# Inverting the attention row sums on VectorE with 32x32 block transposes, in place of logarithm and exponential on ScalarE

## The chip, the cores and the metric

One Trainium2 chip, 8 cores. Each core runs the same program on one element of a batch of 8 (2048 tokens by 1024 features); nothing is passed between cores. The metric is the device time of the slowest core, in microseconds. PE is TensorE, ACT ScalarE, DVE VectorE, POOL GpSimd, SP the engine that issues the DMAs.

## The reference

For each batch element, with E = 1024, 16 heads of 64, T = 2048:

```
xn = layernorm(x)
q, k, v = (xn @ wq.T + bq) / 8, xn @ wk.T + bk, xn @ wv.T + bv
attn = softmax(q @ k.T + causal mask)        # per head, over the keys
s = (attn @ v) @ wo.T + bo
g = silu(xn @ weight.T + pooled(xn) @ disha)
return x + s * g
```

The row sums of the softmax are the denominators that this case is about.

## The kernel before

**Tiling.** Queries are cut into four chunks of 512 (tc 0 to 3), heads into eight pairs (p 0 to 7), keys into blocks of 128. For chunk tc only the first 4 tc + 4 key blocks count. A *unit* is one key block of one pair and chunk: two score matmuls (one per head, 64 rows each) into two PSUM banks of PSS, one exponential on ACT over both into a buffer of PT (six of them), a mask on POOL for blocks on the diagonal, and two value matmuls into the two banks of PSO. Two units are a *batch*. There are 32 pair-and-chunk combinations; k = 8 tc + p counts them.

**Row sums.** The stationary operand of a value matmul is 64 columns of values and 64 columns of ones. So PSO[0:64, 0] holds the unnormalised output of the first head (features by queries), and PSO[64:128, 0] its row sums, the same numbers on all 64 partitions. In bank 1 it is the other way about. Step LNK (L734 to L744) takes the logarithm of both groups of sums on ACT, into the partitions of the outputs they belong to, and one exponential with scale -1 turns them into inverses, in one of two buffers Rb. Step NRM (L691 to L697) multiplies on DVE, once per head (L695, L696), into QA, the input of the output projection. PSO has only one set of banks, so the first value matmul of the next pair waits for both products (L581).

**Fillers.** All other matmuls are *tiles* of 8 matmuls of 512 columns: K, Q, V projections, gate tiles G, output projection O; T is a tile of transposes of the normalised input. They share the two banks of PSF by turns: tile n needs the eviction of tile n - 2 (`bank_free`, L510 to L514 in the tensor program). DVE evicts K (L649), Q (L655), V (L638), O (L669, with two further steps OM at L686 and L690) and most T tiles; ACT evicts G tiles.

**Order.** `schedule()` writes one list of steps, and every engine walks through that list and executes its own steps in that order; there is no other order. Time in it is a count of PE's work (`advance`). `values()` emits PV (the value matmuls of a batch, two batches behind the scores) and, at a pair's end, LNK at once and NRM with a due time 2.3 us later. `evict(n)` puts an eviction into the list right behind its tile's last matmul. Layer norm steps (LNS, LNR, LNA), the sums for the gate weights (WEFF), OM and stores have due times as well; while an NRM is due, most of them are held. Fillers are spread over a pair's batches by ACT's time, save for a block that is put behind the second batch, where the value matmuls of the pair before have just ended: `min(BOUNDARY, 0.45 * quota)` matmuls on top of the share, or 8 where gate tiles stand there. QUOTA is 23, 25, 29 and mostly 37 matmuls a pair for tc 0 to 3. At five places (GATES) ACT changes its table to Silu and back for a burst of G tiles.

Of the kernel before, what the change touches and what calls it, by code (L numbers as in the profile page):

```python
# [6 lines left out]
F32 = mybir.dt.float32  # L7
# [57 lines left out]

GATES = {(1, 5): (0, 1, 2), (1, 7): (3, 4, 5), (2, 2): (6, 7, 8), (2, 7): (9, 10, 11), (3, 1): (12, 13, 14, 15)}

BOUNDARY = 12

WEIGHT = {"T": 2, "LN": 0, "WEFF": 0}  # L70

# [5 lines left out]
def schedule():  # L77

    order, due, tiles = [], [], []
    now = [0.0]  # L80
    burst = [False]
    bs = batches()

    def later(us, *token):
# [2 lines left out]
    def advance(us):  # L87
        now[0] += us
        for d in sorted(x for x in due if x[0] <= now[0]):

            if burst[0] and d[2][0] in ("LNR", "LNA", "XL"):
                continue

            if d[2][0] in ("LNS", "LNA", "WEFF", "WL", "XL") and any(x[2][0] == "NRM" for x in due):
                continue
            due.remove(d)
            order.append(d[2])
# [6 lines left out]
    def evict(n):  # L104
        kind = tiles[n][0]
        order.append(("EV", n) + tiles[n])
        if kind == "Q" and tiles[n][1] * 8 + tiles[n][2] + 3 < 32:
            order.append(("WQK", tiles[n][1] * 8 + tiles[n][2] + 3))
        if tiles[n] == ("Q", 3, 7):
            order.append(("XF",))  # L110
        if kind == "V" and tiles[n][1:] == (NTT - 1, 1):
            order.append(("BO",))
        if kind == "O":
            tt, h = tiles[n][1:]

            wait = max([0.0] + [x[0] - now[0] for x in due if x[2][0] == "NRM"])
            later(wait, "OM", n, tt, h)
            later(wait + 2.2, "ST", tt, h)
            if h == 1 and tt + 2 < 12:
                later(wait + 2.2, "XR", tt + 2)  # L120

    def whole(kind, *which):
        n = tile(kind, *which)
# [6 lines left out]
        evict(n)  # L130

    def ln(tt):
        wait = max([0.0] + [x[0] - now[0] for x in due if x[2][0] == "NRM"])
        later(wait, "LNS", tt)
        later(wait + 2.5, "LNR", tt)
        later(wait + 4.0, "LNA", tt)
        if tt + 2 < NTT:
            later(wait + 5.5, "XL", tt + 2)


    order += [("LNS", 0), ("LNR", 0), ("LNA", 0), ("LNS", 1), ("LNR", 1), ("LNS", 2), ("LNR", 2)]
# [76 lines left out]
    def values(b):  # L218

        tc, p, units = bs[b]  # L220
        order.append(("PV", b))
        advance(sum(2 * (512 - off) for _, _, off in units) / 2400)
        if units[1][1] == 4 * tc + 3:
            k = tc * 8 + p
            order.append(("LNK", k))
            if k < 31:
                later(2.3, "NRM", k)
            return tc, p
        return None

# [2 lines left out]
    for tc in range(NTC):  # L233
        if tc == 3:
            order += [("XR", 0), ("XR", 1)]
        q += fillers(tc)
        for p in range(NPAIR):
            mine = [b for b, x in enumerate(bs) if x[:2] == (tc, p)]
            over += needed(q, [("K", tc, p), ("Q", tc, p)])
            quota = QUOTA[tc][p] - over  # L240

            act = [sum(0.22 + 2 * (512 - off) * 0.83e-3 for _, _, off in bs[b][2]) for b in mine]
            before = (tc, p - 1) if p else (tc - 1, 7)
            extra = 0 if before[0] < 0 else ECH if before in GATES else min(BOUNDARY, 0.45 * max(quota, 0))
            share = [max(quota - extra, 0) * a / sum(act) for a in act]
            due_by, emitted = 0.0, 0
            for i, b in enumerate(mine):
                units = bs[b][2]
                order.extend([("S", b), ("E", b, 0)])
                advance(sum(512 - off for _, _, off in units) / 2400 + 0.2)  # L250
                lag.append(b)
                end = None
                if len(lag) > 2:
                    c, r, old = bs[lag[0]]

                    for u, sc, _ in old:
                        emitted += needed(q, [("V", sc, r // 4)])
                    end = values(lag.pop(0))
                order.append(("E", b, 1))
                if tc == 3 and (p, i) in ((3, 3), (4, 0), (4, 5), (5, 2), (5, 6), (6, 3), (6, 6), (7, 3)):  # L260
                    order.append(("XB",) + xb.pop(0))
                if end in GATES:

                    emitted += needed(q, [("V", 14, 1)]) if tc == 3 and p == 2 else fill(q, ECH)
                    emitted += gate(GATES[end])

                    emitted += fill(q, 5 if tc < 3 else 2)
                due_by += share[i] + (extra if i == 1 else 0)
# [27 lines left out]
def build_program():  # L296
# [46 lines left out]
    o_PT = used  # L343
    PT = [at(f"PT{i}", [NP, 2, 512], F16) for i in range(6)]

    Rb = [at(f"Rb{i}", [NP, 512], F32) for i in range(2)]
    xin = [at(f"xin{i}", [NP, E], F16) for i in range(2)]
    xn = at("xn", [NP, E], F16)
    tri = at("tri_sb", [NP, NP], F16)
# [45 lines left out]
    with ExitStack() as ctx:  # L395
# [16 lines left out]
        s_tile = sem("s_tile")  # L412
        s_ev = {k: sem(f"s_ev{k}") for k in "TVKQGO"}
        s_s, s_exp, s_mask, s_pv = sem("s_s"), sem("s_exp"), sem("s_mask"), sem("s_pv")
        s_lnl, s_rb, s_nrm = sem("s_lnl"), sem("s_rb"), sem("s_nrm")
# [8 lines left out]

        psT = [PSF.ap().bitcast(F16)[:, i, :] for i in range(2)]
        tri2 = bass.AP(tri.ap().tensor, tri.ap().offset, [list(tri.ap().ap[0]), [0, 2], [1, NP]])
        def out_buffer(m):
            return esb[m % 4] if m < 24 else elast[m - 24]

# [77 lines left out]
        def tensor_program(pe):  # L507
# [8 lines left out]
            for t in ORDER:  # L516
# [7 lines left out]
                elif t[0] == "MM":  # L524
                    _, n, a, b = t
                    kind, i, j = TILES[n]
                    if a == 0:
                        bank_free(n)
                        if kind == "V":
                            pe.wait_ge(s_ev["T"], i + 1)  # L530
                            pe.wait_ge(s_wv[j], 16)
                        elif kind in "KQ":
                            pe.wait_ge(s_ev["T"], 4 * i + 4)
                            pe.wait_ge(s_wqk[(8 * i + j) % 3], 16 * ((8 * i + j) // 3 + 1))
                        elif kind == "G":
                            pe.wait_ge(s_weff, 2 * ECH)
                        else:

                            pe.wait_ge(s_nrm, 8 * (i // 4) + 8 - (b < ECH))
                            pe.wait_ge(s_wo, 16)  # L540
                            if bank_of(n) >= 2:
                                pe.wait_ge(s_exp, len(UNITS))
                    elif kind == "O" and i >= 12:
                        pe.wait_ge(s_nrm, 32)
# [27 lines left out]
                elif t[0] == "PV":  # L572
                    tc, p, units = BS[t[1]]
                    for u, sc, off in units:
                        if sc >= 4 * tc:
                            pe.wait_ge(s_mask, int(masks[u]))
                        else:
                            pe.wait_ge(s_exp, u + 1)
                        if sc == 0 and u > 0:

                            pe.wait_ge(s_nrm, 8 * tc + p)  # L581
                        pe.wait_ge(s_ev["V"], nth[tile_no["V", sc, p // 4]] + 1)
                        if u == 0:
                            pe.wait_ge(s_ones, 1)
                        first, last = sc == 0, sc == 4 * tc + 3
                        pe.matmul(PSO[:, 0, off:512], Vp[:, sc, p, 0:128], PT[u % 6][:, 0, off:512],  # L586
                                  start=first, stop=last)
                        pe.matmul(PSO[:, 1, off:512], Vp[:, sc, p, 64:192], PT[u % 6][:, 1, off:512],  # L588
                                  start=first, stop=last).then_inc(s_pv, 1)

        @block.vector
        def vector_program(dve):

            for t in ORDER:
# [96 lines left out]
                elif t[0] == "NRM":  # L691
                    k = t[1]
                    tc, p = k // 8, k % 8
                    dve.wait_ge(s_rb, k + 1)
                    dve.tensor_tensor(QA[tc][0:64, p, :], PSO[0:64, 0, :], Rb[k % 2][0:64, :], ALU.mult)  # L695
                    dve.tensor_tensor(QA[tc][64:128, p, :], PSO[64:128, 1, :], Rb[k % 2][64:128, :],  # L696
                                      ALU.mult).then_inc(s_nrm, 1)  # L697

        @block.scalar
        def scalar_program(act):  # L700
            act.preload_act_table_set(EXP_SET)
            act.wait_ge(s_cst0, 1)
            for t in ORDER:
# [22 lines left out]
                elif t[0] == "E":  # L726
# [3 lines left out]
                    if u >= 6:  # L730
                        act.wait_ge(s_pv, u - 5)
                    act.activation(PT[u % 6][:, :, off:512], PSS[:, 2 * t[2]:2 * t[2] + 2, off:512],  # L732
                                   AF.Exp, bias=neg2[:], scale=0.125).then_inc(s_exp, 1)
                elif t[0] == "LNK":  # L734
                    k = t[1]
                    tc, p = k // 8, k % 8
                    act.wait_ge(s_pv, sum(8 * (4 * c + 4) for c in range(tc)) + (p + 1) * (4 * tc + 4))
                    if k >= 2:
                        act.wait_ge(s_nrm, k - 1)
                    R = Rb[k % 2]  # L740
                    act.activation(R[0:64, :], PSO[64:128, 0, :], AF.Ln)  # L741
                    act.activation(R[64:128, :], PSO[0:64, 1, :], AF.Ln).then_inc(s_lnl, 1)  # L742
                    act.wait_ge(s_lnl, k + 1)
                    act.activation(R[:], R[:], AF.Exp, scale=-1.0).then_inc(s_rb, 1)  # L744

        @block.gpsimd
        def gpsimd_program(pool):
# [82 lines left out]
```

## Time and profile before

| | us |
|---|---|
| median of 3 runs | 613.11 |
| lowest, highest | 582.15, 620.99 |
| profiled execution | 583.26 |
| its span, slowest core | 581.7 |
| spans of the 8 cores | 575.6 to 581.7 |

| engine | busy us | share of the span |
|---|---|---|
| PE | 519.4 | 89% |
| ACT | 398.0 | 68% |
| DVE | 222.9 | 38% |
| POOL | 122.1 | 21% |

The mean granted TensorE clock of the slowest core is 0.991. A matmul's record is longer than the time it holds the engine, since matmuls are pipelined: 512 columns are recorded with 0.38 us, and the next one starts 0.2155 us after it. So the busy share says little on how far PE is from its limit; gaps between starts and the waits say more.

### The profile page before, as it was taken

To read this page: it belongs to the slowest core of one execution; us is meant where nothing else is said; L and a number is where in the kernel's file an instruction comes from. 1 tells how busy PE (TensorE), PEld (TensorE's weight loads), DVE (VectorE), ACT (ScalarE), POOL (GpSimd) and SP (SyncE) were. 2 spreads that over 40 slices of the span, in tenths; PEclk is the share of its full clock that TensorE was granted. 3 is DMA by queue.
4 is the path that set the end of the run, shared out by engine and by line. 5 is a ranking of instruction groups with operands and counts; after the bars stand their busy time and mean duration, and the time that the engine had idled before them with its cause. 6 is when DMAs were issued, how large, how long until landed. Compare 5 with 4: busy or idle time off the path is not lost.

```text
span 581.7 us, 9555 instructions; the slowest of 8 cores (575.6 to 581.7 us)
## 1 busy us (share of the span) xinstructions
PE 519.4 (89%) x2688; PEld 207.9 (36%) x2688; DVE 222.9 (38%) x335; ACT 398.0 (68%) x495; POOL 122.1 (21%) x157
## 2 busy tenths in 40 slices
PE   2889989889979898899999999999998998999896
PEld 1334433333324343333333333433342333333242
DVE  4447566455311230452022212113110635545625
ACT  2256667767655876787688887677748887888650
POOL 0433332221110211011011111010100332252215
PEclk9989999999989999999999999999999999999899
DMA  7933244043111110111010103110205222223113
GB/s 167 282 105 103 91 145 146 19 154 119 37 37 36 38 55 0 55 38 36 1 38 1 42 32 107 39 37 37 74 0 163 72 91 75 91 73 109 61 50 146
DMA packets 17488, 43.68 MB, mean 75 GB/s; under 512 B 2336, under 2 KB 2336, under 8 KB 17056
## 3 DMA queue, kind: packets, MB, share of 16 engines
q1 hardware_dynamic: 17440, 43.07, 23.7%
q8 instruction: 27, 0.44, 0.3%
q14 instruction: 21, 0.17, 0.1%
HBM read 34.67 MB, written 8.39 MB: 74 GB/s over the span
## 4 chain that ended last, share of the span: by engine, by line
PE 62%; ACT 14%; issue 11%; DVE 8%; DMA 3%; POOL 1%; ACTq 0%; SPq 0%; DVEq 0%; POOLq 0%
PE PSF L556 34%; PE PSS L568 10%; PE PSO L586 10%; ACT PT L732 9%; PE PSO L588 7%; DVE QA L696 2%; DVE QA L695 2%; DMA xfirst<-x 2%; DMA wo_sb<-wo 1%; ACT Rb L742 1%; ACT Rb L741 1%; ACT Rb L744 1%; DVE Vp L638 1%; DVE QA L655 1%; PE PSS L556 1%
## 5 line engine op out<-in xcount | busy, mean ns | idle before, releaser
L732 ACT ACTIVATE PT<-PSS,neg 128x1024 f16<-128x1024 f32 (+1 forms) x320 | 299.3, 982 | 110.0 <-PE PSS L568 106.7
L761 POOL TENSOR_TENSOR PT<-PT,tri_sb 128x256 f16<-128x256 f16 x128 | 88.2, 699 | 424.8 <-ACT PT L732 421.0
L556 PE MATMUL PSF<-XG,wqk 128*128 128x512 f16 x512 | 126.2, 383 | 3.9 <-DVE Vp L638 2.2
L586 PE MATMUL PSO<-PT,Vp 128*128 128x512 f16 (+1 forms) x320 | 111.5, 353 | 11.2 <-DVE QA L696 8.9
L568 PE MATMUL PSS<-QA,KT 64*128 64x512 f16 (+3 forms) x640 | 99.4, 353 | 24.4 <-ACT PT L732 17.7
L588 PE MATMUL PSO<-PT,Vp 128*128 128x512 f16 (+1 forms) x320 | 108.9, 350 | 0.0
L556 PEld LDWEIGHTS PSF<-XG,wqk 128*128 128x128 f16 x512 | 49.0, 98 | 58.6 <-issue 7.0
L638 DVE TENSOR_TENSOR Vp<-PSF,bvb 128x512 f16<-128x512 f32 x32 | 22.1, 691 | 117.7 <-PE PSF L556 117.6
L556 PE MATMUL PSF<-wv_sb,XG 128*128 128x512 f16 x256 | 65.9, 384 | 1.1 <-DVE Vp L638 0.7
L568 PEld LDWEIGHTS PSS<-QA,KT 64*128 64x128 f16 x640 | 27.3, 93 | 109.2 <-issue 107.9
L649 DVE TENSOR_SCALAR KT<-PSF,bqk 128x512 f16<-128x512 f32 x32 | 24.0, 750 | 92.4 <-PE PSF L556 92.1
L556 PE MATMUL PSF<-Weff,XG 128*128 128x512 f16 x256 | 56.9, 379 | 2.0 <-DVE Vp L638 1.0
L556 PE MATMUL PSF<-wo_sb,QA 128*128 128x512 f16 x224 | 56.7, 382 | 2.0 <-DMA wo_sb<-wo 1.3
L586 PEld LDWEIGHTS PSO<-PT,Vp 128*128 128x128 f16 x320 | 31.0, 97 | 74.4 <-issue 56.7
L655 DVE TENSOR_SCALAR QA<-PSF,bqk 128x512 f16<-128x512 f32 x32 | 24.0, 750 | 50.5 <-PE PSF L556 50.3
L720 ACT ACTIVATE XG<-PSF 128x512 f16<-128x512 f32 x32 | 19.0, 597 | 30.2 <-PE PSF L556 30.2
L669 DVE TENSOR_TENSOR esb<-PSF,bob 128x512 f32<-128x512 f32 x24 | 16.6, 690 | 55.0 <-PE PSF L556 54.8
L588 PEld LDWEIGHTS PSO<-PT,Vp 128*128 128x128 f16 x320 | 31.4, 98 | 16.0 <-issue 0.7
L556 PEld LDWEIGHTS PSF<-Weff,XG 128*128 128x128 f16 x256 | 24.7, 98 | 33.4 <-issue 4.3
L556 PEld LDWEIGHTS PSF<-wv_sb,XG 128*128 128x128 f16 x256 | 24.7, 99 | 29.6 <-issue 3.8
L556 PEld LDWEIGHTS PSF<-wo_sb,QA 128*128 128x128 f16 x224 | 21.8, 98 | 27.7 <-issue 3.7
L695 DVE TENSOR_TENSOR QA<-PSO,Rb 64x512 f16<-64x512 f32 x32 | 21.7, 679 | 12.6 <-ACT Rb L744 12.5
(39 smaller groups left out, 268.4 us busy)
## 6 DMA issues: line engine op xcount, KB each, us to landing
wqk<-wqk SPq DMA_DIRECT2D x32, 512.0 KB, 3.4
xin<-x SPq DMA_DIRECT2D x24, 256.0 KB, 3.2
out<-esb SPq DMA_DIRECT2D x24, 256.0 KB, 2.0
wbuf<-wT SPq DMA_DIRECT2D x16, 256.0 KB, 3.3
wv_sb<-wv SPq DMA_DIRECT2D x2, 1024.0 KB, 12.3
wo_sb<-wo SPq DMA_DIRECT2D x1, 2048.0 KB, 8.7
out<-elast SPq DMA_DIRECT2D x8, 256.0 KB, 2.4
xfirst<-x SPq DMA_DIRECT2D x4, 256.0 KB, 4.8
```

The source lines that it names most:

```text
L556: ins = pe.matmul(ps(n), l, r, start=ec == 0, stop=ec == ECH - 1)
L568: ins = pe.matmul(PSS[:, 2 * i + h, off:512], KT[64 * h:64 * h + 64, p, sc * NP:(sc + 1) * NP], QA[tc][64 * h:64 * h + 64, p, off:512], st ...
L586: pe.matmul(PSO[:, 0, off:512], Vp[:, sc, p, 0:128], PT[u % 6][:, 0, off:512], start=first, stop=last)
L588: pe.matmul(PSO[:, 1, off:512], Vp[:, sc, p, 64:192], PT[u % 6][:, 1, off:512], start=first, stop=last).then_inc(s_pv, 1)
L638: dve.tensor_tensor(v, ps(n).rearrange("p (a b c) -> p a b c", a=4, b=2), bvb[:, h * 512:(h + 1) * 512].rearrange("p (a b c) -> p a b c", ...
L649: dve.tensor_scalar(KT[:, p, tc * 512:(tc + 1) * 512], ps(n), bqk[:, p:p + 1], None, ALU.add).then_inc(s_ev["K"], 1)
L655: dve.tensor_scalar(QA[tc][:, p, :], ps(n), bqk[:, 8 + p:9 + p], None, ALU.add).then_inc(s_ev["Q"], 1)
L669: dve.tensor_tensor(esb[m % 4][:], ps(n), bob[:, c], ALU.add).then_inc(s_ev["O"], 1)
L695: dve.tensor_tensor(QA[tc][0:64, p, :], PSO[0:64, 0, :], Rb[k % 2][0:64, :], ALU.mult)
L720: act.activation(g, ps(n), AF.Silu).then_inc(s_ev["G"], 1)
L732: act.activation(PT[u % 6][:, :, off:512], PSS[:, 2 * t[2]:2 * t[2] + 2, off:512], AF.Exp, bias=neg2[:], scale=0.125).then_inc(s_exp, 1)
L761: pool.tensor_tensor(a, a, tri2, ALU.mult).then_inc(s_mask, 1)
```

## The change

ACT loses LNK. NRM on DVE becomes seven steps of which six are instructions with work: two block transposes turn the sums over (out of each 32x32 block the first column then holds 32 different sums), a reciprocal works on those 16 columns, and a third transpose, reading each of them 32 times, lays the inverses out over partitions again. Then come the two products. They signal one by one, and the value matmuls of the next pair wait for them one by one. In `schedule()`, NRM stands right behind PV; a flag `soon` holds the steps with due times while the last value matmuls of a pair are near; BOUNDARY is 14; before four of the five gates the block of up to 8 fillers goes.

```diff
-BOUNDARY = 12
+BOUNDARY = 14
@@ advance
-            if d[2][0] in ("LNS", "LNA", "WEFF", "WL", "XL") and any(x[2][0] == "NRM" for x in due):
+            if soon[0] and d[2][0] in ("LNS", "LNR", "LNA", "WEFF", "WL", "XL", "OM", "ST", "XR"):
                 continue
@@ evict (and the same for the steps of ln)
-            wait = max([0.0] + [x[0] - now[0] for x in due if x[2][0] == "NRM"])
-            later(wait, "OM", n, tt, h)
-            later(wait + 2.2, "ST", tt, h)
+            later(0.0, "OM", n, tt, h)
+            later(2.2, "ST", tt, h)
@@ values
-            order.append(("LNK", k))
             if k < 31:
-                later(2.3, "NRM", k)
+                order.append(("NRM", k))
+                soon[0] = False
@@ the loop over batches
+                lag.append(b)
+                soon[0] = len(lag) > 2 and bs[lag[0]][2][1][1] == 4 * bs[lag[0]][0] + 3
                 order.extend([("S", b), ("E", b, 0)])
                 advance(sum(512 - off for _, _, off in units) / 2400 + 0.2)
-                lag.append(b)
@@
                 if end in GATES:
-                    emitted += needed(q, [("V", 14, 1)]) if tc == 3 and p == 2 else fill(q, ECH)
+                    if end == (3, 1):
+                        emitted += needed(q, [("V", 14, 1)])
                     emitted += gate(GATES[end])
@@ buffers
-    Rb = [at(f"Rb{i}", [NP, 512], F32) for i in range(2)]
+    tS = at("tS", [NP, 512], F32)
+    rS = at("rS", [NP, 16], F32)
+    Rb = at("Rb", [NP, 512], F32)
+        spread = bass.AP(rS.ap().tensor, rS.ap().offset, [list(rS.ap().ap[0]), [1, 16], [0, 32]])
@@ tensor program, PV
-                        if sc == 0 and u > 0:
-                            pe.wait_ge(s_nrm, 8 * tc + p)
...
+                        if sc == 0 and u > 0:
+                            pe.wait_ge(s_nrm, 2 * (8 * tc + p) - 1)
                         pe.matmul(PSO[:, 0, off:512], Vp[:, sc, p, 0:128], PT[u % 6][:, 0, off:512],
                                   start=first, stop=last)
+                        if sc == 0 and u > 0:
+                            pe.wait_ge(s_nrm, 2 * (8 * tc + p))
                         pe.matmul(PSO[:, 1, off:512], Vp[:, sc, p, 64:192], PT[u % 6][:, 1, off:512],
@@ vector program, NRM
+                    dve.wait_ge(s_pv, sum(8 * (4 * c + 4) for c in range(tc)) + (p + 1) * (4 * tc + 4))
+                    dve.transpose(tS[0:64, :], PSO[64:128, 0, :])
+                    dve.transpose(tS[64:128, :], PSO[0:64, 1, :]).then_inc(s_turn, 1)
+                    dve.wait_ge(s_turn, k + 1)
+                    dve.reciprocal(rS[:], tS[:].rearrange("p (a b) -> p a b", b=32)[:, :, 0]).then_inc(s_inv, 1)
+                    dve.wait_ge(s_inv, k + 1)
+                    dve.transpose(Rb[:], spread).then_inc(s_rb, 1)
                     dve.wait_ge(s_rb, k + 1)
-                    dve.tensor_tensor(QA[tc][0:64, p, :], PSO[0:64, 0, :], Rb[k % 2][0:64, :], ALU.mult)
+                    dve.tensor_tensor(QA[tc][0:64, p, :], PSO[0:64, 0, :], Rb[0:64, :],
+                                      ALU.mult).then_inc(s_nrm, 1)
@@ scalar program
-                elif t[0] == "LNK":
-                    k = t[1]
-                    tc, p = k // 8, k % 8
-                    act.wait_ge(s_pv, sum(8 * (4 * c + 4) for c in range(tc)) + (p + 1) * (4 * tc + 4))
-                    if k >= 2:
-                        act.wait_ge(s_nrm, k - 1)
-                    R = Rb[k % 2]
-                    act.activation(R[0:64, :], PSO[64:128, 0, :], AF.Ln)
-                    act.activation(R[64:128, :], PSO[0:64, 1, :], AF.Ln).then_inc(s_lnl, 1)
-                    act.wait_ge(s_lnl, k + 1)
-                    act.activation(R[:], R[:], AF.Exp, scale=-1.0).then_inc(s_rb, 1)
```

## Rows read from the trace of the kernel before

**Rows 1.** The page: busy time of PE and ACT, and the chain that ended last.
```profile
PE 519.4 (89%) x2688; PEld 207.9 (36%) x2688; DVE 222.9 (38%) x335; ACT 398.0 (68%) x495; POOL 122.1 (21%) x157
PE 62%; ACT 14%; issue 11%; DVE 8%; DMA 3%; POOL 1%; ACTq 0%; SPq 0%; DVEq 0%; POOLq 0%
```

**Rows 2.** Waits (engine, tile, line <- releaser: us in total, times, longest).
```profile
PE PSS L568 <- ACT PT L732: 17.7, 45, 1.4
...
PE PSO L586 <- DVE QA L696: 8.9, 14, 2.4
...
PE PSS L568 <- DVE QA L655: 5.3, 4, 1.6
...
PE PSF L556 <- DVE Vp L638: 3.9, 6, 0.8
```

**Rows 3.** Groups by form: count | busy us, mean ns | idle us before.
```profile
L655 DVE TENSOR_SCALAR QA<-PSF,bqk 128x512 f16<-128x512 f32 x32 | 24.0, 750 | 50.5 <-PE PSF L556 50.3
L696 DVE TENSOR_TENSOR QA<-PSO,Rb 64x512 f16<-64x512 f32 x32 | 22.2, 694 | 0.4
...
L695 DVE TENSOR_TENSOR QA<-PSO,Rb 64x512 f16<-64x512 f32 x32 | 21.7, 679 | 12.6 <-ACT Rb L744 12.5
L744 ACT ACTIVATE Rb<-Rb 128x512 f32<-128x512 f32 x32 | 20.2, 630 | 3.2 <-ACT Rb L742 0.4
...
L741 ACT ACTIVATE Rb<-PSO 64x512 f32<-64x512 f32 x32 | 19.0, 593 | 10.3 <-PE PSO L588 9.1
L742 ACT ACTIVATE Rb<-PSO 64x512 f32<-64x512 f32 x32 | 18.8, 588 | 0.4
L690 DVE TENSOR_TENSOR esb<-esb,xin 128x512 f32<-128x512 f32 x24 | 18.3, 762 | 4.1 <-DVE esb L686 4.1
...
L618 DVE TENSOR_SCALAR xn<-xin,mv,rstd 128x1024 f16<-128x1024 f16 x12 | 7.4, 614 | 2.0 <-ACT rstd L711 2.0
...
L610 DVE BATCH_NORM_AGGREGATE mv<-st 128x2 f32<-128x12 f32 x16 | 3.3, 209 | 2.6 <-DVE st L606 2.4
```

**Rows 4.** Order of time, 313.7 to 318 us: start, us, engine, line, operands.
```profile
313.75 0.22 PE L588 MATMUL PSO<-PT,Vp 128*128 128x128 f16 x1
...
314.12 0.59 ACT L741 ACTIVATE Rb<-PSO 64x512 f32<-64x512 f32 x1
...
314.94 0.69 DVE L638 TENSOR_TENSOR Vp<-PSF,bvb 128x512 f16<-128x512 f32 x1 [3.96 <-PE PSF L556]
...
316.14 0.68 DVE L695 TENSOR_TENSOR QA<-PSO,Rb 64x512 f16<-64x512 f32 x1 [0.51 <-ACT Rb L744]
316.84 0.69 DVE L696 TENSOR_TENSOR QA<-PSO,Rb 64x512 f16<-64x512 f32 x1
...
317.14 0.61 PE L568 MATMUL PSS<-QA,KT 64*128 64x512 f16 x4
...
317.69 1.11 ACT L732 ACTIVATE PT<-PSS,neg 128x1024 f16<-128x1024 f32 x1 [0.65 <-PE PSS L568]
...
317.78 0.38 PE L586 MATMUL PSO<-PT,Vp 128*128 128x512 f16 x1
```

**Rows 5.** Order of time, 72.6 to 78.3 us.
```profile
72.77 3.40 PE L556 MATMUL PSF<-XG,wqk 128*128 128x512 f16 x15
...
76.75 0.75 DVE L655 TENSOR_SCALAR QA<-PSF,bqk 128x512 f16<-128x512 f32 x1
...
77.75 0.56 PE L568 MATMUL PSS<-QA,KT 64*128 64x512 f16 x4 [1.58 <-DVE QA L655]
```

**Rows 6.** Order of time, 540 to 547.6 us.
```profile
540.09 1.49 DVE L686 TENSOR_TENSOR esb<-esb,XG 128x512 f32<-128x512 f32 x1
541.75 1.39 DVE L690 TENSOR_TENSOR esb<-esb,xin 128x512 f32<-128x512 f32 x1 [0.17 <-DVE esb L686]
...
546.96 0.38 PE L586 MATMUL PSO<-PT,Vp 128*128 128x512 f16 x1 [2.44 <-DVE QA L696]
```

**Rows 7.** Order of time, 565 to 570 us, the kernel's end.
```profile
569.19 0.59 PE L556 MATMUL PSF<-wo_sb,QA 128*128 128x512 f16 x2 [0.69 <-DVE QA L696]
```

More of the change, by code:

```diff
@@ L81, in schedule @@
     burst = [False]
+    soon = [False]
     bs = batches()
@@ L114, in evict @@
             tt, h = tiles[n][1:]
-            wait = max([0.0] + [x[0] - now[0] for x in due if x[2][0] == "NRM"])
-            later(wait, "OM", n, tt, h)
-            later(wait + 2.2, "ST", tt, h)
+            later(0.0, "OM", n, tt, h)
+            later(2.2, "ST", tt, h)
             if h == 1 and tt + 2 < 12:
-                later(wait + 2.2, "XR", tt + 2)
+                later(2.2, "XR", tt + 2)
     def whole(kind, *which):
@@ L132, in ln @@
     def ln(tt):
[L133 to L136, printed above, removed]
+        later(0.0, "LNS", tt)
+        later(2.5, "LNR", tt)
+        later(4.0, "LNA", tt)
         if tt + 2 < NTT:
-            later(wait + 5.5, "XL", tt + 2)
+            later(5.5, "XL", tt + 2)
     order += [("LNS", 0), ("LNR", 0), ("LNA", 0), ("LNS", 1), ("LNR", 1), ("LNS", 2), ("LNR", 2)]
@@ L414, in build_program @@
         s_s, s_exp, s_mask, s_pv = sem("s_s"), sem("s_exp"), sem("s_mask"), sem("s_pv")
-        s_lnl, s_rb, s_nrm = sem("s_lnl"), sem("s_rb"), sem("s_nrm")
+        s_turn, s_inv, s_rb, s_nrm = (sem(n) for n in ("s_turn", "s_inv", "s_rb", "s_nrm"))
         s_mul, s_add, s_addp, s_bog, s_xb = (sem(n) for n in ("s_mul", "s_add", "s_addp", "s_bog", "s_xb"))
@@ L537, in tensor_program @@
                         else:
-                            pe.wait_ge(s_nrm, 8 * (i // 4) + 8 - (b < ECH))
+                            pe.wait_ge(s_nrm, 2 * (8 * (i // 4) + 8 - (b < ECH)))
                             pe.wait_ge(s_wo, 16)
@@ L543, in tensor_program @@
                     elif kind == "O" and i >= 12:
-                        pe.wait_ge(s_nrm, 32)
+                        pe.wait_ge(s_nrm, 64)
                     for ec in range(a, b):
@@ L693, in vector_program @@
                     tc, p = k // 8, k % 8
+                    dve.wait_ge(s_pv, sum(8 * (4 * c + 4) for c in range(tc)) + (p + 1) * (4 * tc + 4))
[5 more added lines that the diff above has]
+                    dve.transpose(Rb[:], spread).then_inc(s_rb, 1)
                     dve.wait_ge(s_rb, k + 1)
-                    dve.tensor_tensor(QA[tc][0:64, p, :], PSO[0:64, 0, :], Rb[k % 2][0:64, :], ALU.mult)
-                    dve.tensor_tensor(QA[tc][64:128, p, :], PSO[64:128, 1, :], Rb[k % 2][64:128, :],
+                    dve.tensor_tensor(QA[tc][0:64, p, :], PSO[0:64, 0, :], Rb[0:64, :],
+                                      ALU.mult).then_inc(s_nrm, 1)
+                    dve.tensor_tensor(QA[tc][64:128, p, :], PSO[64:128, 1, :], Rb[64:128, :],
                                       ALU.mult).then_inc(s_nrm, 1)
```

## The prediction

> **What bounds the kernel now.** I read the page's busy shares and its chain first, then the list of waits, then the groups by form, and then the order of time around one hand-over from a head pair to the next. The page gives TensorE (PE) 89% of the span and ScalarE (ACT) 68%; the chain runs 62% through PE, 14% through ACT, 8% through VectorE (DVE) [rows 1]. So what matters is what makes PE wait. The waits say: 17.7 us for exponentials at the score matmuls (L568), 8.9 us at the value matmuls for the second normalising product (L696), 5.3 us at the score matmuls for an eviction of a Q tile (L655) [rows 2]. DVE itself waits 12.5 us for the inverted sums (L744) [rows 3].
>
> The hand-over at 314 us shows the clean case [rows 4]. The last value matmul of the pair ends at 313.75 + 0.22 = 313.97; call that zero. ACT starts its first logarithm at +0.15. PE meanwhile runs 15 filler matmuls into the two PSF banks, whose tiles have 8 matmuls each, so a tile ends somewhere in them (here after the fourth) and DVE evicts it at 314.94, before the products. The products start at +2.17 and end at +3.56, the next pair's value matmuls start at +3.81: 0.25 after the release. The score matmuls in between started at +3.17 and waited for nothing. ACT, done with its three instructions, runs one exponential and then stands idle 0.65 us. PE loses only some 0.1 us here: the 15 fillers were there to cover the latency, and do.
>
> **What goes from ACT.** 32 times L741, L742, L744 at 0.593 + 0.588 + 0.630 = 1.81 us, 58.0 us in all [rows 3]; ACT falls from 398.0 to 340 us. On PE's path I cost this at nothing: ACT already has idle time behind the three instructions, before the next scores come [rows 4], and in the rest of a pair it works exactly as before. The cover is PE's filler block; if ACT were in fact late there, at most the 17.7 us of waits for exponentials would come back.
>
> **What DVE gets.** Per pair two 64x512 block transposes out of PSUM, a reciprocal on 128x16, one 128x512 transpose, and the same two products. No row shows a DVE transpose. Nearest is L695, 64 partitions by 512 f32 columns out of PSUM, 0.68 us [rows 3]; I take 0.68 for all three. Lower bound: the fastest streaming row, L618, 1024 columns in 0.61, so 0.31 for 512. Upper bound: the slowest 512-column f32 row, 1.39 us [rows 6]. The reciprocal I take at 0.21, like the small aggregate L610 [rows 3]; it cannot be nothing, and a full row would be 0.68. Each step that waits for the one in front costs another 0.17: L690 behind L686 idles 4.1 us in 24 times [rows 3]. So from zero: 0.15, T 0.68 to 0.83, T to 1.53 (0.02 between unlinked ones, as L695 to L696), +0.17+0.21 to 1.91, +0.17+0.68 to 2.76, +0.17+0.68 to 3.61, +0.02+0.69 to **4.32**. DVE busy goes up by 32 x (3 x 0.68 + 0.21) = 72 us to about 295; that is no bound in itself.
>
> The Trainium skill, "VectorE: DVE Perf Modes", section "The three transpose paths", gives 311 ns for a 128x128 bf16 block transpose, and its errata section a fixed part of 151 cycles at 0.96 GHz for one-per-cycle operations. An estimate from these is 311 + 384/0.96 = 711 ns for 512 columns, and 2.5 us more over the kernel than by the row. The same page's "Rules for kernel authors" call the block transpose the fastest within a bank but say to keep the number of chained DVE operations down; here two become six. No row of before can show either.
>
> **The latency alone.** The wait is now split: the first half may start at 3.61 + 0.25 = 3.86, much like 3.81, the second at 4.32 + 0.25 = 4.57. So by latency a pair costs PE about 0.75 us, less where PE's extra fillers (15 become 16 in tc 2 and 17 in tc 3, by min(BOUNDARY, 0.45 quota) and the even share) cover it.
>
> **What is queued behind it.** This is the term that decides. The NRM step used to enter the common order 2.3 us after the values, so that an eviction of a tile ending sooner stood ahead of it on DVE. Now it stands right behind PV in the order, so DVE waits for the last value matmul and then holds everything until 4.32. All evictions of K, Q, V and O tiles of the filler block come behind it. PE has two PSF banks, and `bank_free` makes tile C wait for the eviction of tile A. With r matmuls left in A at zero (1 to 8 alike), B is through at (r + 8) x 0.2155 (15 fillers in a row take 3.40 us with 0.38 for the last [rows 5], so 3.02/14); A's bank is free at 4.32 + 0.02 + 0.75 (L655 [rows 3]) and PE restarts 0.25 later: at **5.34**. PE's order is fixed, so scores and values behind C wait with it. That PE does stand for such an eviction is seen at 76.75: the Q tile's eviction waits behind L696, ends at 77.50, and the score matmuls start at 77.75 after 1.58 us idle [rows 5].
>
> The stall is 5.34 - (r + 8) x 0.2155 where C begins inside the block, else about 0.5 for the split wait:
> - tc 0 and 1, 14 hand-overs without a gate, 15 fillers: C begins for r up to 6 (mean 3.5), stall 2.86; 14 x (0.75 x 2.86 + 0.25 x 0.5) = 31.8.
> - tc 2, 6 of them, 16 fillers: r up to 7 (mean 4), stall 2.75; 6 x (7/8 x 2.75 + 0.06) = 14.8.
> - tc 3, 6 of them, 17 fillers: always, mean r 4.5, stall 2.65; 15.9.
> - 5 gates: the second G tile needs A's bank as well, though ACT evicts the G tiles; 5 x 2.65 = 13.3.
>
> That is 75.8 us, at about 27 places. Off goes what is in the span of before and is now inside or replaced: 8.9 for L696 and 5.3 for L655 [rows 2]. At the end of the kernel the last four O tiles wait for NRM 31; PE idles 0.69 there for L696 already [rows 7], so all of 4.32 in place of 3.56 shows: +0.8. Holding OM, LNS and the like while a hand-over is near (`soon`) spares cases as at 541, where two O steps of 1.49 and 1.39 us stood in front of the products and PE waited 2.44 us [rows 6]; that wait is part of the 8.9. Sum: 75.8 - 8.9 - 5.3 + 0.8 = **+62 us**. The profiled execution took 583.3 us (span 581.7), so 583.3 + 62 = **645 us**. The median of the runs shown is 613.1 (582.2 to 621.0); the profiled one is at their low end, and a median of after may stand above its best in the same way, which the range leaves room for.
>
> The dropped filler block ahead of four gates moves 8 matmuls behind the gate and costs nothing: PE runs G tiles in their place. The two semaphores more, and buffers tS, rS with one Rb in place of two, cost nothing either: the DVE order alone keeps Rb safe. No DMA is moved past another queue's work but the ST and XR issues of O tiles, which no longer wait for NRM.
>
> **Rivals.**
> - *Latency alone.* A's eviction delays nothing, since tiles end late or the banks are ahead. For it: 12 of the 15 fillers can run on two banks. Against: [rows 5]. Price 26 x 0.75 = 19.5, less 8.9: 594 us, within 2%. Chance 0.07.
> - *ACT was the limit (faster).* The mechanism: free of 1.81 us per pair, ACT never makes PE wait and the products come early. It would give back 17.7 + 8.9 = 26.6 us: 557 us. It decides only if the stalls stay under 26.6/27 = 1.0 us, that is if the DVE chain ends by 2.7 us in place of 4.32, for which even transposes of 0.31 (chain end 3.2) are too slow. For it: the chain's 14% through ACT [rows 1]. Chance 0.06.
> - *Quick blocks, or stalls partly absorbed.* Transposes at 0.31 take 3 x 0.37 = 1.1 us off each of 27 stalls: 645 - 30 = 615. Or PE's pause lets ACT get ahead and the 17.7 us go: 627. Chance 0.15.
> - *Slow blocks.* Transposes at 1.39: 3 x 0.71 = 2.1 us more at 27 places, 58 us: 703. Chance 0.06.
> - *The bank wait as summed*, 645 us, between about 630 and 675. Chance 0.66.
>
> The range 612 to 690 takes in the quick and the absorbed case and half the way to the slow one, and leaves out the two others and the far end of the slow one. A measurement tells this kernel from no change at about 2%. Faster 0.06, within 2% 0.06, slower 0.88: the rest and the near-2% edge of the latency case go to slower.
>
> **What would show it.** In the profile of after: three DVE transposes of 0.6 to 0.75 us a pair and the second product ending 4.2 to 4.5 us past the last value matmul; ACT near 340 us busy; PE's waits at the filler matmuls for DVE evictions, now 3.9 us for V tiles [rows 2], at 50 to 80 us in 20 to 27 pieces of 2 to 4 us, with ACT idle longer for scores by as much; waits of score matmuls for exponentials about the same, 15 to 18 us. I am wrong if a transpose is far from 0.68 us, if the PSF waits stay under 20 us, or if the waits for exponentials fall by as much as the PSF waits rise.

## The result and the profile after

The changed kernel takes 691.15 us (median of 4 runs, 686.69 to 696.37), the kernel before 598.0 us (median of 4, 582.15 to 620.99). As a ratio that is **1.187**, 95% interval 1.172 to 1.201; here and below it leaves out executions in which the cores of a die stood at a lower granted clock than the others (here 613 and 621 us of the kernel before, further on 643 and 621 of e8_split and 752 of e11_long_warm), and the kernel before then takes 583 us. The profiled executions are 686.69 and 583.26 us: 103 us more, where the prediction summed 62. The direction and the wait for a bank came out as forecast, the size did not: 691 lies just past the top of the range (690), and a part of it has a cause that the prediction does not name.

The page of after, busy time, granted clock by fortieths of the span, and the chain:

```profile
PE 556.4 (81%) x2688; PEld 213.1 (31%) x2688; DVE 295.8 (43%) x463; ACT 341.4 (50%) x399; POOL 119.9 (18%) x157
...
PEclk9998768999999999999999999999999999999999
...
PE 55%; DVE 21%; issue 12%; ACT 7%; DMA 3%; POOL 1%; DVEq 1%; SPq 0%; ACTq 0%; POOLq 0%
```

ScalarE is at 341 us (340 forecast), VectorE at 296 (295 forecast). DVE has gone from 8% [rows 1] to 21% of the chain, ACT from 14% to 7%.

The waits of after (releaser, us, times, longest); those of before are [rows 2]:

```profile
ACT PT L749 <- PE PSS L573: 247.1, 120, 8.8
...
PE PSF L561 <- DVE KT L657: 22.1, 7, 4.1
PE PSF L561 <- DVE QA L663: 18.2, 6, 4.3
...
PE PSF L561 <- DVE Vp L646: 16.6, 7, 3.7
...
PE PSF L561 <- DVE esb L677: 15.2, 5, 3.4
...
PE PSS L573 <- ACT PT L749: 11.4, 39, 0.6
...
PE PSF L561 <- DVE XG L638: 7.3, 2, 4.2
```

The five PSF lines are the new wait: 79.4 us in 27 places, up to 4.3 us each, where [rows 2] shows 3.9 us for V tiles. With the small ones it is 84 us (6.6 before). TensorE waits there for evictions. Read hand-over by hand-over it is the same sum: TensorE stands for 2.1 to 4.3 us at 27 of the 31 hand-overs (not at k = 6, 10, 11 and 12). ScalarE, freed of some 57 us, waits 247 us for scores, where it waited 106.7 before.

The added instructions (count | busy, mean ns | idle before):

```profile
L704 DVE STREAM_TRANSPOSE tS<-PSO 64x512 f32<-64x512 f32 x32 | 23.0, 718 | 57.7 <-PE PSO L596 57.5
L709 DVE STREAM_TRANSPOSE Rb<-rS 128x512 f32<-128x512 f32 x32 | 22.8, 711 | 3.7 <-DVE rS L707 0.5
...
L707 DVE RECIPROCAL rS<-tS 128x16 f32<-128x16 f32 x32 | 8.1, 253 | 3.3
```

One hand-over (k = 21) in order of time. First VectorE, then TensorE; the last value matmul of the pair ends at 399.36 + 0.22 = 399.58:

```profile
399.69 0.72 DVE L704 STREAM_TRANSPOSE tS<-PSO 64x512 f32<-64x512 f32 x1 [1.05 <-PE PSO L596]
400.42 0.71 DVE L705 STREAM_TRANSPOSE tS<-PSO 64x512 f32<-64x512 f32 x1
401.23 0.25 DVE L707 RECIPROCAL rS<-tS 128x16 f32<-128x16 f32 x1
401.59 0.71 DVE L709 STREAM_TRANSPOSE Rb<-rS 128x512 f32<-128x512 f32 x1
402.40 0.68 DVE L711 TENSOR_TENSOR QA<-PSO,Rb 64x512 f16<-64x512 f32 x1
403.12 0.69 DVE L713 TENSOR_TENSOR QA<-PSO,Rb 64x512 f16<-64x512 f32 x1
403.84 0.75 DVE L657 TENSOR_SCALAR KT<-PSF,bqk 128x512 f16<-128x512 f32 x1
404.51 0.74 DVE L663 TENSOR_SCALAR QA<-PSF,bqk 128x512 f16<-128x512 f32 x1
```

```profile
399.36 0.22 PE L596 MATMUL PSO<-PT,Vp 128*128 128x128 f16 x1
399.41 3.40 PE L561 MATMUL PSF<-XG,wqk 128*128 128x512 f16 x15
404.95 0.38 PE L561 MATMUL PSF<-wv_sb,XG 128*128 128x512 f16 x1 [2.14 <-DVE KT L657]
405.26 0.61 PE L573 MATMUL PSS<-QA,KT 64*128 64x512 f16 x4
405.80 0.39 PE L591 MATMUL PSO<-PT,Vp 128*128 128x512 f16 x1
...
406.52 0.63 PE L596 MATMUL PSO<-PT,Vp 128*128 128x512 f16 x1
406.95 1.49 PE L561 MATMUL PSF<-wv_sb,XG 128*128 128x512 f16 x3
408.37 1.03 PE L573 MATMUL PSS<-QA,KT 64*128 64x512 f16 x4
```

The second product ends at 403.81, 4.23 us past the values (4.32 forecast); the eviction of tile A, in this case of a K tile, goes right behind it; tile C (a V tile) starts at 404.95, 5.37 past the values (5.34 forecast). The second product ends at that distance at 24 of the 31 hand-overs. At the other seven it ends 4.6 to 5.8 us past the values; at six of them other VectorE steps stand in front of the transposes (Weff at 93 us, layer norm at 179 us, steps of an O tile at 566 us), so `soon` does not keep all of them away.

All of this is as the prediction had it, but for those seven. What it did not have at all is in the last lines of the fence: from 406.5 a matmul of 512 columns is recorded with 0.63 us in place of 0.38, three fillers take 1.49 in place of 0.81, four score matmuls 1.03 in place of 0.61. The windows of the same core say why (PEclk, third figure from the end, as a share of full speed):

```profile
399.40:401.50 2.10, 2.10 (x13) 0.99 (x12) 1.68 (x3) 1.25 (x2) 0.00 (x0) 1.00 0.00 0
401.50:404.70 3.20, 1.31 (x7) 0.39 (x4) 2.94 (x5) 0.00 (x0) 0.00 (x0) 1.00 0.24 64
404.70:408.00 3.30, 3.05 (x12) 0.97 (x12) 0.55 (x1) 2.12 (x2) 0.00 (x0) 0.75 0.25 97
408.00:412.00 4.00, 4.00 (x19) 1.22 (x18) 0.00 (x0) 2.41 (x3) 0.00 (x0) 0.78 0.01 4
412.00:416.00 4.00, 3.81 (x22) 1.32 (x20) 0.69 (x1) 2.96 (x5) 2.63 (x4) 1.00 0.00 0
```

Behind the pause the granted clock is at its lower level (1.2 GHz, 0.5 in these terms) for a part of each of the two windows, and back at 2.4 GHz from 412 on. A typical core of after spends 80 us at the lower level (7.5 before); the mean granted clock falls from 0.995 to 0.943. The Trainium skill, "TensorE: Matmul & The Clock Gate", section "Why this matters for your kernels", warns that idle gaps between bursts of matmuls bring the clock back to half rate. The trace agrees on that, with 80 us at the lower level; the gaps that the Trainium skill's row warns of are longer than the 2.14 us here, and the measurement decides.

### The profile page after: what moved, and what is told of

It reads as the page before. It is cut to its first block, busy times and chain, and to the rows that moved or that the text cites. A ratio compares the mean times of both kernels' runs of the same rounds, so it can differ in the third digit from the quotient of the medians.

```text
span 685.0 us, 9620 instructions; the slowest of 8 cores (673.9 to 685.0 us)
## 1 busy us (share of the span) xinstructions
PE 556.4 (81%) x2688; PEld 213.1 (31%) x2688; DVE 295.8 (43%) x463; ACT 341.4 (50%) x399; POOL 119.9 (18%) x157
## 4 chain that ended last, share of the span: by engine, by line
PE 55%; DVE 21%; issue 12%; ACT 7%; DMA 3%; POOL 1%; DVEq 1%; SPq 0%; ACTq 0%; POOLq 0%
PE PSF L561 29%; PE PSS L573 9%; PE PSO L591 9%; PE PSO L596 7%; ACT PT L749 6%; DVE Rb L709 3%; DVE tS L705 3%; DVE tS L704 3%; DVE QA L713 3%; DMA xfirst<-x 1%; DVE QA L663 1%; DMA wo_sb<-wo 1%; DVE rS L707 1%; DVE KT L657 1%; DVE Vp L646 1%
## 5 line engine op out<-in xcount | busy, mean ns | idle before, releaser
L767 POOL TENSOR_TENSOR PT<-PT,tri_sb 128x256 f16<-128x256 f16 x128 | 86.7, 688 | 529.4 <-ACT PT L749 525.6
L561 PE MATMUL PSF<-XG,wqk 128*128 128x512 f16 x512 | 135.6, 401 | 37.7 <-DVE QA L663 12.5
L591 PE MATMUL PSO<-PT,Vp 128*128 128x512 f16 (+1 forms) x320 | 116.8, 369 | 5.1 <-DVE QA L711 3.2
L573 PE MATMUL PSS<-QA,KT 64*128 64x512 f16 (+3 forms) x640 | 102.5, 370 | 15.7 <-ACT PT L749 11.4
L596 PE MATMUL PSO<-PT,Vp 128*128 128x512 f16 (+1 forms) x320 | 114.0, 365 | 1.3 <-DVE QA L713 1.3
L561 PE MATMUL PSF<-wv_sb,XG 128*128 128x512 f16 x256 | 72.8, 412 | 13.6 <-DVE KT L657 5.6
L561 PE MATMUL PSF<-wo_sb,QA 128*128 128x512 f16 x224 | 60.8, 399 | 17.8 <-DVE esb L677 15.2
L561 PE MATMUL PSF<-Weff,XG 128*128 128x512 f16 x256 | 61.5, 401 | 13.9 <-DVE KT L657 5.8
L591 PEld LDWEIGHTS PSO<-PT,Vp 128*128 128x128 f16 x320 | 31.7, 99 | 75.0 <-issue 58.6
L704 DVE STREAM_TRANSPOSE tS<-PSO 64x512 f32<-64x512 f32 x32 | 23.0, 718 | 57.7 <-PE PSO L596 57.5
L596 PEld LDWEIGHTS PSO<-PT,Vp 128*128 128x128 f16 x320 | 32.2, 101 | 19.9 <-issue 6.0
```

The source lines that it names most:

```text
L561: ins = pe.matmul(ps(n), l, r, start=ec == 0, stop=ec == ECH - 1)
L573: ins = pe.matmul(PSS[:, 2 * i + h, off:512], KT[64 * h:64 * h + 64, p, sc * NP:(sc + 1) * NP], QA[tc][64 * h:64 * h + 64, p, off:512], st ...
L704: dve.transpose(tS[0:64, :], PSO[64:128, 0, :])
L767: pool.tensor_tensor(a, a, tri2, ALU.mult).then_inc(s_mask, 1)
```

## The experiments

Theory at this point: T1, the pause for evictions costs 77 us as such; T2, the pauses also bring the clock down, and that is the missing part. The rivals are that the clock falls for another reason, that the chain's latency or VectorE's load is what costs, or that the schedule's other edits do.

**Does the pause bring the clock down?** The changed kernel, with 12 matmuls that nobody reads in front of the second tile that begins behind each hand-over, mostly the one that waits. Nothing else is moved.

```diff
+                if t[0] == "S":
+                    unit = BS[t[1]][2][0][0]
+                elif t[0] == "NRM":
+                    begun = 0
+                elif t[0] == "T" or (t[0] == "MM" and t[2] == 0):
+                    begun += 1
+                    if begun == 2 and t[1] < len(TILES) - 8:
+                        pe.wait_ge(s_exp, unit + 1)
+                        for i in range(12):
+                            pe.matmul(PSS[:, 0, :], KT[:, 0, 0:NP], KT[:, 0, 0:512], start=True, stop=True)
```

> The changed kernel, and at each hand-over 12 matmuls of 512 columns that nobody reads (K values into a free PSS bank) stand in front of the tile that waits for its bank, so that TensorE works through most of its pause. Theory (the pause of about 3 us per hand-over costs twice: once as such, about 83 us, and once because the granted clock falls to the lower level behind it, about 30 us): the pauses for evictions keep their end at 5.33 us past the last value matmul, the mean granted clock rises from 0.94 to above 0.98, slow matmuls (0.63 us recorded) fall from some 180 to under 60, time 650 to 665 us. Rival (the clock falls for another reason, such as DVE transposes out of PSUM or load on all cores): clock stays near 0.94, time 685 to 700 us.

Measured: 663.7 us (663.57 and 663.83), ratio 1.138 where the changed kernel has 1.187, clock 0.995 to 1.0 on all cores. Order of time at the same hand-over:

```profile
382.44 0.22 PE L607 MATMUL PSO<-PT,Vp 128*128 128x128 f16 x1
382.50 3.40 PE L572 MATMUL PSF<-XG,wqk 128*128 128x512 f16 x15
385.74 2.75 PE L532 MATMUL PSS<-KT 128*128 128x512 f16 x12
388.33 0.38 PE L572 MATMUL PSF<-wv_sb,XG 128*128 128x512 f16 x1
388.64 0.61 PE L584 MATMUL PSS<-QA,KT 64*128 64x512 f16 x4
```

Tile C starts no sooner (388.33 is 5.67 us past the last value matmul, where after has 5.37; here, where the pause is one of the shorter, the unread matmuls run a little over its end), and TensorE does 372 matmuls more; yet the kernel is 27 us faster than the changed one, as it keeps its clock. T2 stands. The unread matmuls (with the wait for the bank they write) are the only difference between the two programs, so the 27 us are measured, not argued (23 us if the two profiled executions are taken). The unread matmuls cost something too: the four hand-overs without a pause get 12 of them as well, 4 x 12 x 0.2155 = 10 us. An estimate of the clock's whole price is thus 27 + 10 = 37 us.

**Do the other edits cost, and what is ScalarE's relief worth?** The inversion is left out; the products use a constant.

```diff
-                    dve.transpose(tS[0:64, :], PSO[64:128, 0, :])
-                    dve.transpose(tS[64:128, :], PSO[0:64, 1, :]).then_inc(s_turn, 1)
...
-                    dve.transpose(Rb[:], spread).then_inc(s_rb, 1)
-                    dve.wait_ge(s_rb, k + 1)
+                    if k == 0:
+                        dve.memset(Rb[:], 0.001).then_inc(s_rb, 1)
+                    dve.wait_ge(s_rb, 1)
```

> The changed kernel without the inversion: the transposes and the reciprocal are left out and the products use a constant. This shows what ScalarE's relief of 58 us is worth by itself and what is left of the schedule edits. Theory (bank wait): the products end at 1.5 us, tile C's bank is free at 2.5, waits for PSF evictions fall under 12 us, clock above 0.985, time 570 to 582 us. Rival (ScalarE had been a limit): 557 us or less. Rival (the schedule edits themselves, BOUNDARY, held steps, cost the time): over 620 us.

Measured: 580.5 us, ratio 0.996 (0.994 to 0.998). Its waits:

```profile
ACT PT L745 <- PE PSS L573: 164.6, 108, 8.2
...
PE PSS L573 <- ACT PT L745: 15.1, 49, 0.8
```

So BOUNDARY, the held steps, the gates and the relief of ScalarE come to nothing together: with all of the inversion gone the kernel gains 2.5 us. One run does not tell a cost of the edits from an equal gain by the relief, but the waits name no such pair: those for exponentials are 15.1 us where [rows 2] has 17.7, those for the products are gone (8.9 before), those of fillers for VectorE are 13 where the kernel before has 6.6. Taking 58 us from ScalarE is worth next to nothing. This bounds every way of moving the inversion under this schedule. And it adds up: e1_warm has 372 x 0.2155 = 80 us of unread matmuls and 16 us of waits of fillers for VectorE, 83 us more than the 13 here, and 580.5 + 83 is its 663.7.

**Is it what stands behind NRM, or the transposes?** Logarithm and exponential back on ScalarE, everything else as changed. Of the edit only the place in the order is shown, against the changed kernel.

```diff
             k = tc * 8 + p
+            order.append(("LNK", k))
             if k < 31:
                 order.append(("NRM", k))
```

> The arithmetic of before (logarithm and exponential on ScalarE) under the changed schedule: VectorE stands at the products from the last value matmul to 3.56 us, as it waits for ScalarE, and the evictions stand behind it. Theory (what costs is what is queued behind the waiting NRM step, whoever inverts): tile C's bank is free at 3.56+0.02+0.75+0.25 = 4.58 us, 27 pauses of about 2.3 us, 60 us, with some clock loss: 640 to 665 us. Rival (the transposes' own work is what costs): within 2% of 583 us.

Measured: 652.1 us, clock 0.970 (median of the cores), waits of TensorE:

```profile
PE PSF L559 <- DVE KT L655: 18.1, 7, 3.6
PE PSF L559 <- DVE QA L661: 16.3, 6, 4.1
...
PE PSF L559 <- DVE Vp L644: 12.7, 7, 3.1
PE PSF L559 <- DVE esb L675: 11.3, 5, 2.7
```

Not one transpose on VectorE, and 69 us slower than the 583.0 of before. Two thirds of the loss come with the place in the order alone: VectorE stands at an instruction that waits for another engine, and the evictions stand behind it.

**And the reverse: the transposes under the schedule of before.** Shown against the kernel before; the NRM step itself is that of the changed kernel.

```diff
-            order.append(("LNK", k))
             if k < 31:
                 later(2.3, "NRM", k)
```

> The block transposes on VectorE under the schedule of before: NRM 2.3 us later in the order, evictions of earlier tiles in front of it, BOUNDARY 12, the filler block in front of gates back. Theory: the pause moves from tile C to the value matmuls: chain from 2.3 to about 6.4 us, value matmuls at 6.7 in place of 3.8; waits for PSF evictions under 15 us, waits for the products 60 to 75 us, clock 0.93 to 0.95 again since the pauses are as long; 665 to 690 us. Rival (the place of NRM in the order is the whole cause and the chain itself is cheap): under 610 us.

Measured: 675.6 us, clock 0.949. Now the value matmuls wait:

```profile
PE PSO L589 <- DVE QA L709: 53.6, 25, 4.5
...
PE PSO L594 <- DVE QA L711: 6.9, 20, 0.4
```

The place in the order is not the whole cause either. The 4.1 us of VectorE work have to lie between two value matmuls on the one set of PSO banks; in one piece, either the evictions wait for them or the value matmuls do.

**Someone else evicts.** ScalarE takes the first tile that ends behind a hand-over, if K or Q.

```diff
+                elif t[0] == "EV" and t[2] in "KQ" and t[1] in by_act:
+                    _, n, kind, tc, p = t
+                    act.wait_ge(s_tile, n + 1)
...
+                        act.activation(KT[:, p, tc * 512:(tc + 1) * 512], ps(n), AF.Identity,
+                                       bias=bqk[:, p:p + 1]).then_inc(s_ev["K"], 1)
```

> The changed kernel, and the first tile that ends behind each hand-over is evicted by ScalarE if it is a K or Q tile (20 of 31; about 15 of these hand-overs pause now). The VectorE chain is untouched. Theory (bank wait): the pauses go where ScalarE evicts and stay at the 12 hand-overs whose first tile is V, T or O, so about 40 us of pauses in place of 83, clock near 0.97, 625 to 650 us. Rival (the chain's latency costs, whoever evicts): 680 us or more.

Measured: 641.7 us (639.67 and 643.68), clock 0.964. In its waits K and Q are all but gone from the PSF lines (0.9 us for VectorE, 2.5 for ScalarE, where after has 40 us) and what VectorE still evicts is left:

```profile
PE PSF L570 <- DVE Vp L655: 19.0, 8, 3.6
PE PSF L570 <- DVE esb L686: 15.1, 5, 3.4
```

The VectorE chain is as long as before, and 50 us are back. The pause is the bank's, not the latency's.

**The chain cut open.** The changed kernel, with two transposes right behind the values, reciprocal and third transpose 1.2 us later, the products 2.3 us later; BOUNDARY 14 in e6_between, 18 in e7_between18.

```diff
-                order.append(("NRM", k))
+                order.append(("INV1", k))
+                later(1.2, "INV2", k)
+                later(2.3, "NRM", k)
```

> The same seven VectorE steps cut in three entries of the order: two transposes right behind the last value matmul, reciprocal and third transpose 1.2 us later, the products 2.3 us later, so that evictions of tiles that have ended by then stand in between. Theory: tile C's bank is free at about 2.6 us or, for late ends, 3.7; pauses for PSF evictions under 25 us in all, the second product ends at about 5 us, value matmuls wait about 1 us per hand-over, no pause is longer than 2 us so the clock stays above 0.98; 595 to 615 us. Rival (the added 72 us of VectorE work cannot be hidden in any order): over 650 us.

> e6_between with BOUNDARY 18 in place of 14. Theory: more fillers cover the later products where the quota allows (chunks 2 and 3 only, since 0.45 of the quota binds before): waits for the products fall by 5 to 10 us, and as much may come back as score matmuls waiting for exponentials; within 8 us of e6_between. Rival: more fillers run into tile C and D and pause there, 10 us or more slower.

Measured: 615.8 us (a little above the range) at a clock of 0.981, and 620.3 us. In e6_between the PSF waits are 17 us in all, the waits for the products 10, and those for exponentials 21.8:

```profile
PE PSS L575 <- ACT PT L755: 21.8, 43, 3.5
...
PE PSO L593 <- DVE QA L717: 6.2, 8, 2.0
```

Same instructions, same VectorE work, 75 us less than the changed kernel: by far most of its loss (75 of 108 us) is order. It is still 5% behind the kernel before. More fillers (e7) do not help: the waits for the products stay at 10 us, where 5 to 10 us less were expected, and those for exponentials rise by 2.4.

**One edit alone, on the kernel before: the split wait.** The first product signals too, which the cut does not show.

```diff
+                        if sc == 0 and u > 0:
+                            pe.wait_ge(s_nrm, 2 * (8 * tc + p) - 1)
                         pe.matmul(PSO[:, 0, off:512], ...
+                        if sc == 0 and u > 0:
+                            pe.wait_ge(s_nrm, 2 * (8 * tc + p))
                         pe.matmul(PSO[:, 1, off:512], ...
```

> The kernel before with one edit of the change, the split wait: each product signals by itself and the first value matmul waits for the first product only. Theory: up to 0.5 us at those of the 14 hand-overs where TensorE waits for the second product (8.9 us in all), so 3 to 6 us faster, 577 to 580 us, ratio 0.990 to 0.995. Rival (that time comes back as a wait of the second half): no change.

Measured: ratio 0.9975, interval 0.9947 to 1.0003: no gain that can be told from none, where 3 to 6 us were expected. The waits for the products did fall, from 8.9 to 3.9 us; in the profiled execution other waits took their place (wo_sb's DMA 4.1 us for 1.3, exponentials 19.0 for 17.7), as the rival had it. With e2_noinv, which leaves the inversion out, at 0.996, none of the runs points to a version that beats both kernels, and the kernel before stays the best.

**How pause and clock go with the chain's length.** Without the reciprocal and the third transpose (the products use the turned sums; so part of the computation is left out), and with the third transpose twice:

```diff
-                    dve.wait_ge(s_turn, k + 1)
-                    dve.reciprocal(rS[:], tS[:].rearrange("p (a b) -> p a b", b=32)[:, :, 0]).then_inc(s_inv, 1)
-                    dve.wait_ge(s_inv, k + 1)
-                    dve.transpose(Rb[:], spread).then_inc(s_rb, 1)
```

That is a part of e9_short's edit; this is one of e10_long's:

```diff
+                    dve.transpose(Rb[:], spread).then_inc(s_rb, 1)
+                    dve.wait_ge(s_rb, 2 * k + 2)
```

> The changed kernel without the reciprocal and the third transpose: the products use the turned sums themselves (that part of the computation is left out). The chain ends about 1.15 us earlier, at 3.1 us. Theory (each pause is chain end + 1.09 - where tile B ends, so it moves one for one with the chain; the clock follows the pauses): 27 x 1.15 = 31 us less pause and 10 to 15 us less for the clock, 640 to 652 us, clock near 0.97. Rival (a fixed price per hand-over, whatever the chain's length): above 670 us.

> The changed kernel with the third transpose done twice, one behind the other: the chain ends 0.8 us later, at 5.05 us. Theory: 27 x 0.8 = 22 us more pause; the clock is at the lower level behind nearly every pause already, so it adds 5 us or less: 708 to 722 us, clock 0.92 to 0.94. Rival (the clock's loss grows with the pause's length): above 728 us.

Measured: 627.05 us and 734.5 us. Both misses, and in the same way: a chain 1.15 us shorter gave 64 us, not 41 to 46, and one 0.8 us longer cost 43 us, not 27. The median of each die, first of e9_short, then of e10_long:

```profile
die 0 (median of its cores): 616.2 us, clock 0.987
die 1 (median of its cores): 618.2 us, clock 0.987
```

```profile
die 0 (median of its cores): 723.1 us, clock 0.910
die 1 (median of its cores): 726.6 us, clock 0.896
```

The pauses move one for one with the chain (table below), the clock moves much more. My expectation that the clock was low behind nearly every pause already was wrong. Counted in the traces, the pauses with a stretch at 1.2 GHz right behind them are, by core, 2 to 6 of 27 in e9_short, 8 to 12 in e3_order, 17 to 22 in after and 26 or 27 in e10_long, where many of the stretches are also longer. A last run gives e10_long 15 matmuls that nobody reads:

> e10_long (third transpose twice) with 15 matmuls that nobody reads in front of the tile that waits, as in e1_warm with 12. Theory (all that grew more than the chain in e10_long is TensorE at its lower clock): clock above 0.985, and the time is that of e1_warm plus the 27 x 0.8 = 22 us of longer pauses: 680 to 692 us. Rival (long chains cost through something else too, such as VectorE falling behind with layer norm): over 700 us at a clock above 0.98.

Measured: 694.9 us (one execution), clock 0.992; 3 us above the range. That is 40 us under e10_long's 734.5, and 31 above e1_warm, where 22 were expected. Its 93 unread matmuls more are 20 us, its fillers wait 5 us longer for VectorE (21 against 16) and its value matmuls 2 us longer for the products. The extra of long pauses is the clock, but for these few us.

All of it together. Chain end is when the second product ends past the last value matmul, at the hand-over of k = 21; waits are of the slowest core (of core 0 for e10_long), time at 1.2 GHz the median over the cores:

| kernel | chain end | fillers wait for DVE | time at 1.2 GHz | us |
|---|---|---|---|---|
| e2_noinv | 1.6 | 13 | 8 | 580.5 |
| e9_short | 3.1 | 51 | 18 | 627 |
| e3_order | 3.6 | 68 | 40 | 652 |
| after | 4.2 | 84 | 80 | 691 |
| e10_long | 5.1 | 106 | 133 | 734 |
| e1_warm (after, TensorE kept busy) | 4.2 | 16 | 5 | 664 |
| e11_long_warm | 5.1 | 21 | 12 | 695 |

Where TensorE is kept busy, the wait is filled and not gone, so the fourth column says what counts in those two. In the others, 567 us (e2_noinv less its waits) plus the waits leaves 9, 17, 40 and 61 us for 18, 40, 80 and 133 us at the lower level: 0.4 to 0.5 each. The 40 us for after agree with the 37 from e1_warm.

## Why the prediction failed where it did

- **What bounds before, and what the relief is worth: right.** ScalarE's 58 us were costed at nothing; e2_noinv has 2.5 us for the relief and for no chain at all.
- **The chain: right.** 4.32 us summed, 4.23 measured. A transpose takes 0.71 to 0.72, not 0.68, the reciprocal 0.25, not 0.21; a dependent step costs 0.10 where 0.17 was taken, and that pays for both. The Trainium skill's "VectorE: DVE Perf Modes", "The three transpose paths", had led to an estimate of 711 ns; L709 shows 711 and L704 718, so the Trainium skill's figure for a smaller block, stretched to 512 columns, was nearer than the row of a neighbouring operation. (The 151 cycles that the prediction names beside it stand in the Trainium skill for an fp32 tensor_tensor add; the 711 does not use them.)
- **What is queued behind it: right in place and count, a little small in size.** C starts at 5.37 past the values (5.34); the forecast had 75.8 us at about 27 places, the trace has 27 (the five gates among them, as forecast), with 84 us of waits by the profile. The r matmuls left in tile A were taken as spread evenly; where a T tile of 0.6 us takes B's place C stands sooner and waits longer (4.28 us at 42 us, 4.07 at 161). And other VectorE steps get in the way, in front of the chain (the seven late ends above) or between it and the eviction (two Weff steps, 1.29 us, at 148 us, where C waits 4.19). This term was too small by 8 us.
- **Off went 14.2 us; about that went.** Waits for the products fell from 8.9 to 4.5, those for Q evictions at the score matmuls from 5.3 to 3.2, those for exponentials from 17.7 to 11.4: 12.8 in all. One term made up for another.
- **The clock: missing.** The step that failed is the sum itself, "75.8 - 8.9 - 5.3 + 0.8 = +62 us": it priced a pause of TensorE at its length, and every rival's price was worked out in the same way, at full clock. e1_warm puts a figure on what was left out: 27 us of the difference of 108 between 691 and 583, and about 37 with the 10 us of unread matmuls that filled no pause. With 37, 645 would have been 682, and with the pauses 8 us larger 690, where 691 was measured.
- **It could have been read before.** The kernel before has one pause of over 2 us at a hand-over, the 2.44 us of [rows 6]. Its trace goes on (the first fence TensorE's order of time, the second the windows, granted clock third from the end):

```profile
547.49 0.63 PE L586 MATMUL PSO<-PT,Vp 128*128 128x512 f16 x1
...
548.34 1.49 PE L556 MATMUL PSF<-wo_sb,QA 128*128 128x512 f16 x3
549.76 1.04 PE L568 MATMUL PSS<-QA,KT 64*128 64x512 f16 x4
```

```profile
547.00:550.40 3.40, 3.40 (x11) 0.87 (x11) 1.08 (x2) 0.00 (x0) 0.00 (x0) 0.54 0.07 24
```

  Matmuls at half rate right behind the pause, for 3.3 us. A forecast that puts 27 such pauses into a kernel should have asked what the one that is there does.
- **The rivals.** "Latency alone" (594) is refuted by e5_actev, where the chain is as long and 50 us are back, "ACT was the limit" (557) by e2_noinv. "Partly absorbed" has no sign: waits for exponentials fell by 6.3 us while PSF waits rose by 77. The upper end of the range came from slow transposes (703); the time went there by another road, so that 691 lies so near the range is luck.

What stays open: why the clock goes to the lower level behind some pauses of 2 to 3 us and not behind others. e9_short has 27 pauses of 1.9 us on average and 18 us at the lower level, e10_long 27 of 3.9 us and 133. Nor was it always one long pause: the kernel before has a stretch at a granted clock of 0.50 from 165.0 to 168.4 us behind two waits of TensorE of 0.91 and 0.84 us.

## What to carry to other kernels

In an in-order engine, cost an instruction that waits by what stands behind it: here a 4.2 us chain at the head of VectorE's queue held evictions that TensorE needed, and its place in the order was worth more (75 us of the 108) than the work in it. With two banks in turn, such a hold, with the eviction behind it, may last no longer than one tile plus what is left of the one before (this is the prediction's sum for the stall, turned round; no run was made to test it). And price a pause of TensorE at its length plus about half of the time at half clock behind it, after looking in the trace of before for what its own longest pauses were followed by; an engine that is not the limit (here ScalarE, relieved of some 57 us) gives next to nothing back.

## What the runs showed of the hardware

- A block transpose on VectorE of 512 f32 columns takes 0.71 to 0.72 us, on 64 partitions out of PSUM and on 128 out of SBUF alike, also when it reads each of 16 columns 32 times; a reciprocal on 128x16 takes 0.25 us.
- A pause of 2.1 us by the profile was followed by stretches at 1.2 GHz; 12 matmuls of no use in front of the waiting tile, 372 in all, made the kernel 27 us faster. Each us at 1.2 GHz cost 0.4 to 0.5 us of time.
- The clock's loss grows faster than the pauses: 51, 68, 84, 106 us of waits went with 18, 40, 80, 133 us at the lower level.
